# A node's sums of graph layer two merged on the lane, gathered as one row instead of two

## What is computed

```
def gat_conv(x, W, attn_l, attn_r, src, dst, n_nodes):
    feat = (x @ W).reshape(n_nodes, H, D)
    e = leaky_relu(el[src] + er[dst], NEG_SLOPE)
    m = segment_max(e, dst)
    ex = exp(e - m[dst])
    denom = segment_sum(ex, dst)
    out = segment_sum((ex / denom[dst])[:, :, None] * feat[src], dst)
xn = layernorm(x)
x = x + gat_conv(elu(gat_conv(xn, layer 1)), layer 2) + linear_attention(xn)
x = x + ffn(layernorm(x))     # 8 experts, two hidden layers, all nodes through all experts
```

## Time and profile before

| | us |
|---|---|
| three runs | 3247.24, 3247.81, 3248.17; median 3247.81 |
| profiled execution, first to last instruction | 3526.7 |
| of it: node and index pass, to the first blocks | 0 to 385 |
| layer one | 385 to 1688 |
| hidden pass and start of layer two | 1688 to 1990 |
| layer two with experts | 1990 to 3527 |

### The profile page before, as it was taken

The page is one execution under the profiler, slowest core; times in us unless marked ns, Lnnn a source line. Parts: engine busy times, 40 slices in busy tenths (PEclk is TensorE's granted clock), DMA queues, the critical chain, the costliest instruction groups (busy, mean ns, idle before and its releaser), DMA issues. The chain is left out here.

```text
span 3526.7 us, 33756 instructions
## 1 busy us (share of the span) xinstructions
PE 2158.3 (61%) x7294; PEld 1353.6 (38%) x7294; DVE 2302.8 (65%) x5558; ACT 1906.1 (54%) x6229; POOL 2134.4 (61%) x2028
## 2 busy tenths in 40 slices
PE   6700455555544454544581006888898888888999
PEld 5600333333333332333361003544454444554565
DVE  7882788888988888888563235655466554665631
ACT  3300778787867667766462224544455444554532
POOL 3337677777767777764475666666666666666200
PEclk9855566666755555555796557989898998989999
DMA  6413899999989999998544465555565555555310
GB/s 230 122 21 103 312 338 345 341 348 337 374 330 364 369 345 358 364 348 318 156 127 116 151 226 186 163 167 177 177 190 160 171 173 174 188 171 169 136 33 12
DMA packets 244661, 783.82 MB, mean 222 GB/s; under 512 B 70282, under 2 KB 118253, under 8 KB 217801
## 3 DMA queue, kind: packets, MB, share of 16 engines
q0 software_dynamic: 127664, 369.53, 33.2%
q1 hardware_dynamic: 86715, 391.15, 29.1%
q10 hardware_dynamic: 30078, 20.99, 2.4%
HBM read 404.26 MB, written 378.13 MB: 222 GB/s over the span
## 5 line engine op out<-in xcount | busy, mean ns | idle before, releaser
L1514 POOL DMA_INDIRECT e_rows<-scratch_table,k_src x1664 | 1742.9, 1047 | 816.0 <-issue 400.3
L1624 DVE SCALAR_TENSOR_TENSOR e_ring<-e_ring,k_same,e_rows 128x520 f32<-128x520 f32 (+1 forms) x1560 | 967.6, 620 | 505.0 <-ACT e_rows L1647 179.0
L1647 ACT ACTIVATE e_rows<-e_rows 128x64 f32<-128x64 f32 (+1 forms) x4160 | 1196.9, 371 | 36.4 <-issue 24.9
L2251 PE MATMUL e_p_y<-e_wfo,e_h 128*121 128x256 f32 x1664 | 418.3, 407 | 116.4 <-DVE e_y L2013 67.6
L2251 PEld LDWEIGHTS e_p_y<-e_wfo,e_h 128*121 128x121 f32 x1664 | 325.8, 198 | 224.9 <-issue 128.5
L2225 PE MATMUL e_p_a<-e_xt,e_wf 128*128 128x484 f32 x832 | 387.4, 611 | 10.2 <-ACT e_h L2160 6.5
L2160 ACT ACTIVATE e_h<-e_p_a,e_shift,e_scale 128x484 f32<-128x484 f32 x208 | 151.9, 749 | 435.0 <-remote 282.5
L2237 PE MATMUL e_p_b<-e_h,e_wf 128*128 128x484 f32 x832 | 362.6, 578 | 13.8 <-ACT e_h L2160 11.5
L2013 DVE SCALAR_TENSOR_TENSOR e_y<-e_p_y,e_w,e_y 121x256 f32<-121x256 f32 x416 | 181.0, 476 | 248.5 <-PE e_p_y L2251 101.1
L1017 PE MATMUL e_p_kv<-e_wkv,nd_feat 128*121 128x512 f32 x208 | 190.0, 1066 | 107.2 <-DVE nd_feat L922 73.5
L1593 DVE TENSOR_TENSOR e_rows<-e_rows,e_shared 128x4096 f32<-128x4096 f32 x52 | 229.7, 4416 | 22.5 <-issue 8.9
(11 more groups left out here) (438 smaller groups left out, 3569.4 us busy)
## 6 DMA issues: line engine op xcount, KB each, us to landing
scratch_rows_a<-e_ring SPq DMA_DIRECT2D x104, 2112.0 KB
scratch_sums<-e_ring SPq DMA_DIRECT2D x104, 1032.0 KB
e_rows<-scratch_table,k_src POOLq DMA_INDIRECT x1664
scratch_table<-na_frow ACTq DMA_DIRECT2D x52, 245.8 KB
scratch_table<-hi_frow ACTq DMA_DIRECT2D x52, 124.8 KB
na_x<-in_x SPq DMA_DIRECT2D x13, 484.0 KB
e_wkv<-in_x SPq DMA_DIRECT2D x52, 121.0 KB
scratch_res<-e_wkv SPq DMA_DIRECT2D x52, 121.0 KB
```

What stands on the lines that cost most here:

```text
L1514: nc.gpsimd.indirect_dma_start(out=rows[:, n % B, g, :], out_offset=None, in_=table, in_offset=bass.IndirectOffsetOnAxis(ap=k.src[:, n * G ...
L1624: nc.vector.scalar_tensor_tensor(ring[:, i, j - c0, 0:W + H], prev, k.same[:, n * G + j:n * G + j + 1], rows[:, rb, j, 0:W + H], ALU.mult, ...
L1647: last = nc.scalar.activation(rows[:, rb, j, at], rows[:, rb, j, at], ACT.Copy, scale=rows[:, rb, j, W + h:W + h + 1])
L2251: last = nc.tensor.matmul(self.p_y[bank][0:BK, i * D:(i + 1) * D], self.h2[:, e % 2, kt, v:v + BK], self.wfo[:, e, kt, :], start=kt == 0, ...
```

## The change

Layer two's edge pass uses `MergedTails` as well, on a new DRAM table `rows_b` with the sums and, behind each group's, its 128 merged rows. `Tails` loses what only layer two used (its own table, the rows of "none", their stores). The experts gather one row a node tile, 4 instead of 8 a group, at the even steps 0 to 6 of the same block; POOL issues the head gather of a group besides, and at the end the last group's head gather stands between the node gathers of groups 11 and 12. `below` and its exponential go, `shares` is a reciprocal and a product, and a join is one fused multiply and add. `index_pass` works out three values a node: layer one's place serves both layers.

```
-            c(V.tensor_tensor(place[:, 2, :], xp[:, BK:2 * BK], has[:, :], ALU.mult))
-            c(V.tensor_copy(place[:, 4, :], has[:, :]))
-            for i in (1, 4):
-                c(V.tensor_tensor(w[:, i, :], lane[:, 1, :], lane[:, 0, :], ALU.is_gt))
-                c(V.tensor_tensor(w[:, i + 1, :], lane[:, 1, :], z3[:, 2, :], ALU.is_gt))
+            c(V.tensor_copy(place[:, 2, :], has[:, :]))
+            c(V.tensor_tensor(w[:, 1, :], lane[:, 1, :], lane[:, 0, :], ALU.is_gt))
+            c(V.tensor_tensor(w[:, 2, :], lane[:, 1, :], z3[:, 2, :], ALU.is_gt))
...
-            for i in range(5):
+            for i in range(3):
                 last = nc.tensor.transpose(p_r[0:BK, i * NB:(i + 1) * NB], place[:, i, :], k.ident[0:NB, 0:NB])
...
-                                                 (a["table2"], a["er2"], k.starts2, 1, a["sums2"], CAP))
+                                                 (a["table2"], a["er2"], k.starts2, 1, k.sums2, RP))
...
-        tails = MergedTails(nc, a, k, L, s, sums, stored) if L is L1 else Tails(nc, a, k, L, s, k.tails2)
+        tails = MergedTails(nc, a, k, L, s, sums, stored)
...
-            if n == NB:
-                self.tails.sync_out(sp, Q - 1)
+            if n < NB + 2:
+                self.tails.sync(sp, n)
...
-        src = self.k.tails2[0:1 + (g + 1) * TR, :] if j else self.a["sums2"][0:(g + 1) * CAP, :]
-        nc.gpsimd.indirect_dma_start(out=self.rows[:, i, j, :], out_offset=None, in_=src,
-                                     in_offset=bass.IndirectOffsetOnAxis(
-                                         ap=self.index[:, 2 + j, g * KB + i:g * KB + i + 1], axis=0)
-                                     ).then_inc(self.rows_in[i], 16)
+        self.nc.gpsimd.indirect_dma_start(out=self.rows[:, i, :], out_offset=None, in_=self.k.sums2[0:(g + 1) * RP, :],
+                                          in_offset=bass.IndirectOffsetOnAxis(
+                                              ap=self.index[:, 1, g * KB + i:g * KB + i + 1], axis=0)
+                                          ).then_inc(self.rows_in[i], 16)
 
     def pool(self, pool, n, j):
-        if n % PB == 0 and n >= 2 * PB and j < 2 * KB:
-            self.gather(pool, n // PB - 2, j // 2, j % 2)
+        if n % PB == 0 and n >= 2 * PB and j % 2 == 0 and j < 2 * KB:
+            self.gather(pool, n // PB - 2, j // 2)
 
     def pool_last(self, pool):
         for g in (Q - 2, Q - 1):
+            if g == Q - 1:
+                self.tails.gather(pool, g)
             for i in range(KB):
-                for j in range(2):
-                    self.gather(pool, g, i, j)
+                self.gather(pool, g, i)
...
-    def below(self, dve, g):
...
+    def shares(self, dve, g):
+        nc, rec = self.nc, self.rec
         for i in range(KB):
-            dve.wait_ge(self.rows_in[i], 32 * (g + 1))
+            dve.wait_ge(self.rows_in[i], 16 * (g + 1))
         c = self.join_steps(dve, g, 0)
...
+        c(nc.vector.reciprocal(rec[:, :], self.rows[:, :, L2.den]))
         c.done()
         c(nc.vector.tensor_tensor(rec[:, :], rec[:, :], self.has[:, g * KB:(g + 1) * KB], ALU.mult))
         c.done()
...
-        c(nc.vector.tensor_tensor(rows[:, i, :, 0:D], rows[:, i, :, 0:D], broad(self.q[:, i, :], D), ALU.mult))
         if i == 0:
             dve.wait_ge(self.res_in[g % 3], 16 * (g // 3 + 1))
-        c.done()
-        c(nc.vector.tensor_tensor(y, rows[:, i, 0, 0:D], y, ALU.add))
-        c.done()
-        nc.vector.tensor_tensor(y, rows[:, i, 1, 0:D], y, ALU.add).then_inc(self.joined, 1)
+        nc.vector.scalar_tensor_tensor(y, self.rows[:, i, 0:D], self.rec[:, i:i + 1], y, ALU.mult, ALU.add
+                                       ).then_inc(self.joined, 1)
...
-            if kq == 2 and j == 4:
-                act.wait_ge(self.d_ready, g + 1)
-                wait(act, self.joined, KB * g)
-                nc.scalar.activation(self.sc[:, :, :], self.d[:, :, :], ACT.Exp).then_inc(self.sc_ready, 1)
```

More of the change, by code:

```diff
@@ L465, in index_pass @@
         lack = s.sb("lack", [NB, BK])
-        w = s.sb("w", [NB, 6, BK])
-        place = s.sb("place", [NB, 5, BK])
+        w = s.sb("w", [NB, 4, BK])
+        place = s.sb("place", [NB, 3, BK])
         took = s.sb("took", [P, 4, Q, J], I32)
@@ L720, in _ @@
             c(V.tensor_tensor(z3[:, 0, :], z3[:, 0, :], w[:, 3, :], ALU.subtract))
             c.done()
-            c(V.tensor_tensor(place[:, 3, :], w[:, 1, :], has[:, :], ALU.mult))
-            c(V.scalar_tensor_tensor(z3[:, 0, :], w[:, 4, :], 1.0, z3[:, 0, :], ALU.add, ALU.mult))
+            c(V.scalar_tensor_tensor(z3[:, 0, :], w[:, 1, :], 1.0, z3[:, 0, :], ALU.add, ALU.mult))
             c.done()
@@ L728, in _ @@
             dve.wait_ge(turned, 1)
-            c(V.tensor_copy(k.index[:, :, :], p_r[0:BK, 0:4 * NB].rearrange("p (a n) -> p a n", a=4)))
-            c(V.tensor_copy(k.has[:, :], p_r[0:BK, 4 * NB:5 * NB]))
+            c(V.tensor_copy(k.index[:, :, :], p_r[0:BK, 0:2 * NB].rearrange("p (a n) -> p a n", a=2)))
+            c(V.tensor_copy(k.has[:, :], p_r[0:BK, 2 * NB:3 * NB]))
             c.done()
@@ L1154, in __init__ @@
         self.spread, self.cb_ready = s.sem("carry_spread"), s.sem("cb_ready")
-        self.out, self.none_set = s.sem("tail_out"), s.sem("none_set")
+        self.out = s.sem("tail_out")
         self.at_s, self.at_g, self.at_d, self.at_c = 0, P, P + 8, P + 16
[L1158 to L1162, removed]
-        c.done()
-        nc.vector.memset(self.tl[0:1, L.max:L.row], -BIG).then_inc(self.none_set, 1)
     def scalar_keep(self, act, q, final):
@@ L1289, in scalar @@
             self.scalar_carry(act, q)
[L1291 to L1314, removed]
 class MergedTails(Tails):
@@ L1836, in __init__ @@
         R = L2.row
-        self.index = s.sb("index", [BK, 4, NB], I32)
+        self.index = s.sb("index", [BK, 2, NB], I32)
         self.has = s.sb("has", [BK, NB])
@@ L1847, in __init__ @@
         self.shift = s.sb("shift", [P, 2, E * 2])
[L1848 to L1852, removed]
+        self.rows = s.sb("grow", [BK, KB, R])
         self.rec = s.sb("grec", [BK, KB])
@@ L1940, in sync_last, with gather @@
             self.sync(sp, n, 0)
-            if n == NB:
-                self.tails.sync_out(sp, Q - 1)
+            if n < NB + 2:
+                self.tails.sync(sp, n)
             self.sync(sp, n, 1)
         sp.wait_ge(self.y_out, 16 * Q)
-    def gather(self, pool, g, i, j):
-        nc = self.nc
-        if i == 0 and j == 0:
+    def gather(self, pool, g, i):
+        if i == 0:
             pool.wait_ge(self.stored[0], 16 * PB * (g + 1))
@@ L2068, in spread @@
         nc = self.nc
-        c = self.join_steps(dve, g, 18)
+        c = self.join_steps(dve, g, 6)
         c.done()
@@ L2082, in norm @@
         for i in range(KB):
-            nc.vector.tensor_scalar(self.rows[:, i, 0, 0:D], self.y[:, g % 3, i, :], self.mv[:, i, 0:1], self.rstd[:, i:i + 1],
+            nc.vector.tensor_scalar(self.rows[:, i, 0:D], self.y[:, g % 3, i, :], self.mv[:, i, 0:1], self.rstd[:, i:i + 1],
                                     ALU.subtract, ALU.mult).then_inc(self.xn_ready, 1)
@@ L2129, in vector @@
         if kq == 2:
-            if j == 3:
-                self.below(dve, g)
             if j == 7:
@@ L2265, in turn @@
                 last = nc.tensor.transpose(self.p_u[i // 2][:, at:at + BK],
-                                           self.rows[:, i, 0, mt * P:(mt + 1) * P], k.ident[0:BK, 0:BK])
+                                           self.rows[:, i, mt * P:(mt + 1) * P], k.ident[0:BK, 0:BK])
             if i % 2:
@@ L2344, in gps_kernel @@
         k.sums1 = scratch("rows_a", (Q * RP, L1.row))
-        k.tails2 = scratch("tails_b", (NROW, L2.row))
+        k.sums2 = scratch("rows_b", (Q * RP, L2.row))
         k.iota = k.sb("iota", [P, P])
@@ L2348, in gps_kernel @@
         k.ident = k.sb("ident", [P, P])
-        k.index = k.sb("index", [BK, 4, NB], I32)
+        k.index = k.sb("index", [BK, 2, NB], I32)
         k.slot = k.sb("slot", [P, Q], I32)
```

42 lines of the change are left out of this document (7 added, 35 removed).

## The result

The changed kernel takes 3204.0 us (median of 4 runs, 3202.2 to 3206.3) where the kernel before took 3247.5 (3246.3 to 3248.2, 4 runs on the same chip): a ratio of 0.9869, 95% interval 0.9855 to 0.9882, 43.5 us less. The forecast was 3228, 20 less than before. The time lies inside the range (3201 to 3258), at its lower end, where rival B (POOL the pace throughout) had put it with a chance of 0.13 and a time of 3203.

The account below looks back on a forecast made before the run. The prediction took PE to set most of the pace, with POOL's late gathers costing 16 us. Its terms summed as 3247.8 - 3 (index pass) - 16 (POOL) - 13 (start) + 12 (new chain) = 3228 us, range 3201 to 3258.

Parts of the forecast that it names:

- rival B: Layer two: POOL was the pace throughout, the 45 us lie before layer two; -44, about 3203, chance 0.13.
- What bounds the kernel now: Prediction's opening part: rebuilt layer two's rounds; PE's path 3232, POOL's 3293, against 3247.8 measured.
- Index pass: Index pass: 12 fewer DVE operations, two fewer transposes and a narrower copy, counted in full; -3 us.
- POOL per round: Layer two: four gathers out, one head gather in, so the wait for POOL ends; -16 us, bounds 0 to -44.
- Start of the experts: Layer two, group 0: PE starts its expert products 13 us earlier, and all its rounds with it; -13.
- DVE, -3.5 a round at nothing: Layer two's joins and merge: DVE gains 3.5 us a round, covered by PE's waits; costed at nothing beyond the start.
- The new chain: Layer two: node gathers wait for merge and store, DVE stands at `shares` about 10 us a round; +12, 0 to 28.
- The head gather's wait for its stores: Layer two on POOL: the head gather waits for its group's stores, about 4 us a round, covered.
- A: POOL never was the pace; the 16 is PE's coupling with ACT and DVE and stays; likeliest 3240, chance 0.25.
- C: Slower: DVE's wait at `shares` for merge, store and gathers makes PE stop; 3287 or 3271, chance 0.17.
- The rule of the Trainium skill: About 2.0 us fixed per gather, nearly all completion, about 50 ns dispatch; POOL hardly notices four gathers a round; 3244.

Follow-up runs that it names:

- near_less3: Changed kernel with node gathers issued one behind the other and twelve row gathers a round left out in layer two; 3113.9 us.
- b_plain: The kernel before, with no edit, profiled again; 3245.8 us in one run, profiled span 3244.0.
- b_half: Kernel before without the four gathers a round of the tails' rows, a constant in their place; 3192.7 us, ratio 0.982.
- near_nohead: Changed kernel with node gathers one behind the other and no head gather in layer two; 3166.7 us, ratio 0.9751.
- a_dup: Changed kernel with four more node gathers a round, of the same rows into a tile nobody reads; 3248.9 us.
- near_late: Changed kernel with node gathers one behind the other, those of the first group alone issued eight row gathers later; 3182.5 us, ratio 0.9798.
- a_dve: Changed kernel with about the old join's DVE work put back, on a tile nobody reads; 3246.0 us, ratio 0.9995 to the kernel before.
- a_less1: Changed kernel with four of 64 row gathers a round left out in layer two behind the first two blocks; 3176.7 us.
- a_near: Changed kernel with its four node gathers a round issued one behind the other, without row gathers between; 3181.5 us, ratio 0.9799.
- a_waits: Changed kernel, both layers, every second row gather waiting for its own and its neighbour's sum, the others for nothing; 3203.4 us.

## Why the prediction was wrong

**The step that failed** is the weighing at the end of "What bounds the kernel now": "I take it that PE sets most of the pace and that POOL's late gathers cost the 16; POOL's rows overstate it by 4%, or stages before layer two are shorter in the runs." Both rounds had been rebuilt to within two microseconds: TensorE's 86 is 85.9 (`near_less3`), POOL's 92 is 93.8 (the node gather's 1.34 stands, the row gather's 1.25 is 1.278 on the mean). The larger of the two, 3293, was set aside because it missed the measured 3247.8 by 45. The error was not in POOL's rows but in the start that it was counted from: 1884.1, taken from a profile with 279 us of stalls, is 1815.5 in a clean one. The second half of the sentence, "or stages before layer two are shorter", was the right one, and it was priced, as rival B. The prediction had rebuilt the rounds of layer two because of the stalls, and taken its start as it stood. What the runs showed in its place: POOL set the pace of layer two before the change (`b_plain`, `b_half`), and the term that the sum has at -16 is -45, of which a new wait takes 15 back. That the time fell inside the range is partly luck, as the last paragraph of this section says.

Point by point:

- *Index pass, -3.* Right. POOL's wait for the chain went from 62.4 to 59.6, -2.8; at the first row gather of layer two, behind all of layer one, 1.6 of it are left. `b_plain`, then after:

```profile
L413 POOL DMA_INDIRECT scratch_starts<-nd_er,k_index x52 | 60.7, 1167 | 77.9 <-DVE at_ones L732 62.4 <-issue 15.5
```

```profile
L411 POOL DMA_INDIRECT scratch_starts<-nd_er,k_index x52 | 60.9, 1171 | 75.1 <-DVE at_ones L719 59.6 <-issue 15.5
```

- *POOL per round, -16 (0 to -44).* Mis-sized. 4 x 1.344 out and 1.24 in is 4.1 a round, 45 over 11, at the bound that was named; 1.4 a round comes back as the wait for the merged rows (below), so 30 remain between the first and the last row gather. `b_half` (-56), `near_nohead` (-14.8) and `a_dup` (+45, or 59 less the wait used up) show it from three sides.
- *Start of the experts, -13.* It happened: from the first row gather to the first expert product 213.5 us (2029.0 - 1815.5) became 201.0 (2014.9 - 1813.9), -12.5. As a term it was wrong: with POOL the pace, a later start is made up (`near_late`). What the change gains behind the last row gather, 11.7, is of the same size and probably the same cause, a join four steps later in DVE's order and its last gather earlier in POOL's, but of the last groups; no run takes that apart.
- *DVE, -3.5 a round at nothing.* Wrong as a statement, though nothing is missing from the sum for it. The clause on PE's waits, which "cover the gain", holds only outside the loop from merge to merge. `a_dve` puts 4.5 us a round of it back and the whole gain goes. With the old join's work the change gains nothing: the two DVE operations that each join lost made the room that the merge took.
- *The new chain, +12 (0 to 28).* The links were nearly right: 18 us from merge to `shares` (19.6 in the changed kernel, 18.0 in `a_less1`), DVE standing for 10 (100.2/9 = 11.1 a round, where 8.4 in `below` were there before). The cost, 15 on POOL (1.4 x 11), or the 22.5 that `a_near` gets back, lies in the range, but not where it was looked for: it is not TensorE that stops (31.9 us, less than before), it is POOL that waits for the store. It was taken for a delay hung on to the round, and is a loop with a period of its own, 91.3, which the changed kernel runs at.
- *The head gather's wait for its stores, covered.* Right: 0.30 in front of each.

Of the rivals, B is what happened before the change: POOL was the pace throughout. That its 3203 meets 3204.0 within 1 us is luck: it had -44 for POOL and nothing else, and what it left out, the new wait (+15), the stretch behind the last row gather (-12) and the start (-2), nearly cancels. A falls with `b_half`. C's chain exists and, closed into a loop, sets the changed kernel's rounds, but only 1.4 above POOL's; it costs more when POOL gets faster (`a_less1`) or DVE does more (`a_dve`). That TensorE stops for it, as C had it, did not happen. The rule of the Trainium skill (DMA: Bandwidth & Descriptors, "Anatomy of one DMA — SWDGE (gpsimd) path") would have left four gathers a round nearly free and the time at 3244; POOL's rows and `b_half` decide against it for this kernel.

## What to carry to other kernels

When a profiled execution is slower than the runs, the stalls can lie in any stage: a path counted from a start time out of it carries all the stalls ahead of that start, and a path that comes out too long by about their size is not refuted. Divide the length of a round by the count of an engine's instructions, gaps included, before trusting its busy share: POOL was 76% busy and full. And when one engine's work is cut, look for the loops of nearly the same length (here 91.3, 89.9 and 85.9 a round): they say how much of the gain is to be had, and which two edits are worth more together than the sum of each alone (`a_less1` 27, `a_near` 22, both 68).

## What the runs showed of the hardware

The 0.30 us in front of each indirect gather on POOL is not a wait for a semaphore: it stood there when the profile named DVE, when it named issue, and when every second row gather waited for no semaphore at all (`a_waits`: 176.2 us in front of 578 row gathers, where the changed kernel has 176.5 in front of 579). What makes it is not shown. With a mean of 0.97 (layer two's rows) to 1.04 (a node's) of busy time, POOL gives out one gather of 121 to 128 rows every 1.28 us (rows) to 1.34 (a node's), as long as it waits for nothing; over the nine rounds of the thirteen profiles compared here the means are 1.27 to 1.29 and 1.33 to 1.38.
